# Attention probabilities turned by DMA instead of TensorE, two heads at a time, and the output projection in four parts

## The chip, the cores and the metric

The kernel runs on one core of a Trainium2 chip. The metric is the device time of one execution in microseconds (us); less is better. The engines are TensorE (PE in the profile), VectorE (DVE), ScalarE (ACT), GpSimd (POOL) and SyncE (SP), which issues the DMAs. Each engine has a queue of instructions that it executes in order, and semaphores are all that ties the queues together.

## The reference

One block of a transformer: cross-attention with a residual, then a mixture of experts with a residual. The part that matters, cut down:

```
B, L, D = 8, 128, 256            # T = 128 context tokens; 16 heads of 128, 4 key/value heads
xn = layernorm(x)
q = rope(rms_norm(xn @ wq));  k = rope(rms_norm(xn @ wk));  v = xn @ wv
k_ctx = rms_norm(ctx @ wk_ctx);  v_ctx = ctx @ wv_ctx
k_full, v_full = concat([k_ctx, k]), concat([v_ctx, v])      # 256 keys
scores = q . k_full / sqrt(128) + causal mask on the own keys
probs = softmax(scores);  x1 = x + (probs . v_full) @ wo
xn2 = layernorm(x1)
out = x1 + shared expert(xn2) + top-2 of 8 experts(xn2)
```

## The kernel before, in words

The batch has eight rows b of 128 tokens. Each row has four groups g, one per key/value head, of four query heads each; u = 4b + g counts the groups. Rows 0 and 7 are written out, rows 1 to 6 are a loop on every engine. Behind row 7 comes the tail: router, shared expert and eight experts for two halves of the tokens.

Products keep nearly fp32 precision by splitting each operand into an fp16 high part and an fp16 low part: ScalarE rounds (`..._copy`), VectorE makes the rest (`..._low`, `low()`), and TensorE adds three products. In one group the steps are:

- `scores(b, g)`: four heads against 256 keys into `sc_ps`, with the mask (L1267, L1289).
- VectorE takes the maximum and the bias (L941, L945), ScalarE the four exponentials with their sums `den` (`exps`, L524) into `probs`, fp32.
- `normalise` on VectorE divides `probs` by `den` (L950, L953).
- `turn_probs` (called in the group behind): eight fp32 transposes of 128x128 on PE into `pt_ps` (L1300), `p_copy` and `p_low` round them to `pT_hi` and `pT_lo`.
- `mix`: six matmuls of 512 columns, values stationary, into `o_ps`, which holds the output with the head dimension on the partitions (L1310); `o_copy` and `o_low` round it to `oT_hi`, `oT_lo`.
- `out_proj(b - 1)`: all 48 matmuls of the row before against wo, in group 1 (L1324), into `proj[0]`; then `residual` and, in group 2, `second_norm` on VectorE, with `l2_root` on GpSimd between them.

Between these run the preparations of what comes next: `q_turn` (PE), `q_copy`, `q_low` of the next group; `q` (projection), rotation, `q_squares`, `q_roots`, `q_add` two groups ahead; in group 0 the value projections `vc` and `v`; in group 1 the next row's input: `ln_scale` (DVE), `ln_high` (ACT, L435 with the tile x_hi), `ln_low` (POOL, L712), `turn_inputs` (PE, L1182, L1185), `in_copies`; in group 2 the next row's keys: `kc`, `k`, `k_squares`, `kc_squares`, `k_roots`, `kc_roots`, `kc_scale`, `k_add`, `k_scale`; in group 3 `kc_turn`, `k_turn`, `kc_copy`, `k_copy`, `kc_low`, `k_low`. Every order is written by hand, once per engine, in functions called `row`. There is no planner. `kc` uses the bank `turn`, which all turned inputs and queries share too.

The core of PE's order in group 1 of a row inside the loop:

```
scores(b, 1); q_turn(b, 2); turn_probs(b, 1); q(b, 3)
out_proj(b - 1); turn_inputs(b + 1)
mix(u - 1, 0)
```

## Time and profile before

| | us |
|---|---|
| three runs | 376.12, 376.57, 378.42 (median 376.57) |
| the profiled execution, its own time | 377.97 |
| its span, first to last instruction | 376.3 |
| PE, PE weight loads, DVE, ACT, POOL busy | 343.7, 237.3, 325.6, 271.2, 165.8 |
| mean granted clock of PE | 0.977 |
| DMA, share of 16 engines | 11.0% |

The profile's times come from one execution. PE busy counts matmuls, whose ends are modelled: a matmul's duration holds a tail of about 0.17 us that the next one overlaps, so work on PE is better read from starts than from durations. A granted clock of 1.0 is 2.4 GHz, 0.5 is 1.2 GHz. "Idle before" with an arrow names what ended an engine's wait.

### The profile page before, as it was taken

How to read it: one execution, taken by the hardware profiler on the slowest of the kernel's cores; microseconds unless marked ns; L12 is line 12 of the kernel's file. 1: busy time of each engine (PE TensorE's matmuls, PEld its weight loads, DVE VectorE, ACT ScalarE, POOL GpSimd, SP SyncE). 2: the span in 40 equal slices, each digit the busy share in tenths (PEclk: the TensorE clock that was granted, in tenths of full speed). 3: DMA queues.
4: the chain of work that ended last, by engine and by line, in shares of the span. 5: the costliest groups of instructions: out<-in, count | busy, mean ns of one | idle time of the engine just before them, and what ended most of it. 6: DMA issues, size and time to landing. Idle time of an engine off the chain costs nothing.

```text
span 376.3 us, 7781 instructions
## 1 busy us (share of the span) xinstructions
PE 343.7 (91%) x2471; PEld 237.3 (63%) x2476; DVE 325.6 (87%) x625; ACT 271.2 (72%) x913; POOL 165.8 (44%) x242
## 2 busy tenths in 40 slices
PE   6697798799999999999999999999999999998994
PEld 5373555376567665866685577567666778674572
DVE  1668999998999899899989998999899897759653
ACT  3557879676986797699759876986797567167562
POOL 3356565652754275427344443644174300334330
PEclk9788989999999999999999999999999999989999
DMA  5967000000030003000000000000000000000011
GB/s 179 379 212 223 17 0 2 1 2 14 3 111 0 14 0 111 14 1 0 0 14 0 0 0 14 0 0 0 0 0 1 2 0 2 2 0 3 22 35 57
DMA packets 11603, 13.49 MB, mean 36 GB/s; under 512 B 824, under 2 KB 9024, under 8 KB 11584
## 3 DMA queue, kind: packets, MB, share of 16 engines
q1 hardware_dynamic: 11584, 13.25, 11.0%
q8 instruction: 10, 0.16, 0.2%
q14 instruction: 9, 0.07, 0.1%
HBM read 12.20 MB, written 1.05 MB: 35 GB/s over the span
## 4 chain that ended last, share of the span: by engine, by line
PE 40%; DVE 24%; ACT 17%; issue 10%; POOL 4%; DMA 2%; SPq 1%; DVEq 1%; ACTq 0%; POOLq 0%
PE proj L1324 10%; ACT probs L524 8%; PE pt_ps L1300 5%; DVE probs L953 5%; PE proj L1157 4%; PE turn L1246 3%; DVE nmax L941 3%; DVE pT_lo L879 3%; PE o_ps L1310 3%; POOL q_rot L744 3%; PE sc_ps L1267 2%; ACT pT_hi L435 2%; DMA wq<-in_L_xattn_wq_dram 2%; ACT q_junk L468 2%; DVE q_t L870 2%
## 5 line engine op out<-in xcount | busy, mean ns | idle before, releaser
L524 ACT ACTIVATE probs<-sc_ps,nbias,q_r 128x256 f32<-128x256 f32 x128 | 70.8, 574 | 2.8 <-DVE nbias L945 2.8
L744 POOL TENSOR_TENSOR q_rot<-q_t 128x512 f32<-128x512 f32 x32 | 41.4, 1295 | 42.8 <-DVE q_t L872 42.0
L953 DVE TENSOR_SCALAR probs<-probs,rden 128x256 f32<-128x256 f32 x128 | 51.2, 461 | 1.1
L1157 PE MATMUL proj<-wq_hi,xT 128*128 128x512 f16 x128 | 40.1, 396 | 2.9 <-DVE wq_lo L863 2.9
L435 ACT ACTIVATE pT_hi<-pt_ps 128x512 f16<-128x512 f32 x64 | 34.8, 597 | 10.9 <-PE pt_ps L1300 10.9
L468 ACT ACTIVATE q_junk<-proj 128x128 bf16<-128x128 f32 x128 | 34.0, 295 | 11.7 <-DVE q_t L872 11.7
L879 DVE SCALAR_TENSOR_TENSOR pT_lo<-pt_ps,pT_hi 128x512 f16<-128x512 f32 x64 | 41.0, 682 | 0.6 <-ACT pT_hi L435 0.6
L941 DVE TENSOR_REDUCE nmax<-sc_ps 128x4 f32<-128x1024 f32 x32 | 38.9, 1214 | 1.5 <-PE sc_ps L1289 1.5
L831 POOL TENSOR_TENSOR wq<-xn_all,weight 128x512 bf16<-128x512 f32 x16 | 17.1, 1074 | 44.1 <-DVE weight L1098 23.4
L1324 PE MATMUL proj<-wo_hi,oT_hi 128*128 128x256 f16 x128 | 34.9, 273 | 0.0
L1324 PE MATMUL proj<-wo_lo,oT_hi 128*128 128x256 f16 x128 | 34.9, 273 | 0.0
L1324 PE MATMUL proj<-wo_hi,oT_lo 128*128 128x256 f16 x128 | 34.9, 273 | 0.0
L1300 PE MATMUL pt_ps<-ident,probs 128*128 128x128 f32 x256 | 34.2, 278 | 0.3
L701 POOL TENSOR_TENSOR q_r<-q_me,power 128x4 f32<-128x4 f32 x32 | 33.3, 1042 | 2.5
L435 ACT ACTIVATE qT_hi<-turn 128x512 f16<-128x512 f32 x32 | 19.5, 610 | 19.9 <-PE turn L1246 19.9
L1300 PEld LDWEIGHTS pt_ps<-ident,probs 128*128 128x128 f32 x256 | 29.5, 143 | 0.8 <-DVE probs L953 0.5
L1246 PE MATMUL turn<-ident,q_rot 128*128 128x128 f32 x128 | 19.8, 277 | 10.6 <-POOL q_rot L744 4.9
L468 ACT ACTIVATION_READ_ACCUMULATOR q_junk<-proj 128x1 f32 x128 | 28.5, 227 | 0.0
L524 ACT ACTIVATION_READ_ACCUMULATOR probs<-sc_ps,nbias,q_r 128x1 f32 x128 | 27.6, 215 | 0.0
L1310 PE MATMUL o_ps<-pT_hi,v_hi 128*128 128x512 f16 x64 | 24.3, 379 | 3.2 <-DVE pT_lo L879 3.2
L879 DVE SCALAR_TENSOR_TENSOR oT_lo<-o_ps,oT_hi 128x512 f16<-128x512 f32 x32 | 21.9, 686 | 5.8 <-ACT oT_hi L435 5.8
L1267 PE MATMUL sc_ps<-kT_hi,qT_hi 128*128 128x256 f16 x128 | 24.5, 273 | 0.5 <-ACT probs L524 0.2
(216 smaller groups left out, 920.7 us busy)
## 6 DMA issues: line engine op xcount, KB each, us to landing
wq<-in_L_xattn_wq_dram SPq DMA_DIRECT2D x4, 512.0 KB, 9.1
w<-in_L_ffn_w_dram SPq DMA_DIRECT2D x2, 1024.0 KB, 10.5
wq<-in_L_xattn_wo_dram SPq DMA_DIRECT2D x1, 2048.0 KB, 8.2
ctx_b<-in_ctx_dram SPq DMA_DIRECT2D x8, 128.0 KB, 2.1
out_dram<-x_all SPq DMA_DIRECT2D x4, 256.0 KB, 2.2
x_all<-in_x_dram SPq DMA_DIRECT2D x1, 896.0 KB, 12.3
wkc<-in_L_xattn_wk_ctx_dram SPq DMA_DIRECT2D x1, 512.0 KB, 4.2
wk<-in_L_xattn_wk_dram SPq DMA_DIRECT2D x1, 512.0 KB, 5.1
```

What stands on the lines that cost most here:

```text
L435: return nc.scalar.activation(out_, in_, ACT.Copy, scale=scale)
L468: last = nc.scalar.activation(junk[:, head], bank[:, head], ACT.Square, scale=scale, accum_out=dst[:, h:h + 1])
L524: last = nc.scalar.activation(probs[:, h, :], sc_ps[:, h, :], ACT.Exp, bias=nbias[:, h:h + 1], scale=q_r[:, g, h:h + 1], accum_out=den[:, ...
L701: nc.gpsimd.tensor_tensor(r, me, power[:], ALU.pow).then_inc(root, 1)
L744: nc.gpsimd.tensor_tensor(q_rot[:], q_t1[:], q_t2[:], ALU.add).then_inc(q_added, 1)
L879: return nc.vector.scalar_tensor_tensor(out=lo, in0=src, scalar=scale, in1=hi, op0=ALU.mult, op1=ALU.subtract)
L941: nc.vector.tensor_reduce(nmax[:], sc_ps[:], AX_X, ALU.max, negate=True).then_inc(s_max, 1)
L953: last = nc.vector.tensor_scalar(probs[:, h, :], probs[:, h, :], rden[:, h:h + 1], None, ALU.mult)
L1157: last = nc.tensor.matmul(bank[:], xT[:, a, c, :], w[:, c, cols], start=(n == 0), stop=(n == 3 * DC - 1))
L1300: last = nc.tensor.transpose(pt_ps[:, a, h * P:(h + 1) * P], probs[:, h, a * P:(a + 1) * P], ident[:])
L1310: last = nc.tensor.matmul(o_ps[:], v[:, a, g * P:(g + 1) * P], p[:, a, :], start=(a == 0 and i == 0), stop=(a == 1 and i == 2))
L1324: last = nc.tensor.matmul(proj[0][:, 0:D], o[:, h // R, (h % R) * P:(h % R + 1) * P], w[:, h, :], start=(h == 0 and i == 0), stop=(h == H ...
```

## The change

- ScalarE no longer leaves the probabilities whole: `p_round` rounds `probs`, undivided, to fp16 `p_hi`, two heads at a time; the first pair stands between the third and the fourth exponential. `p_rest` on VectorE makes `p_lo`. `normalise`, `turn_probs` on PE, `p_copy` and `p_low` are gone.
- SP issues four transposing DMAs per group, high and low of each pair (128 x 512 fp16), to `pT_hi` and `pT_lo` (two slots).
- `mix` has the probabilities stationary and 128 columns of values moving: 24 matmuls. Its result has the tokens on the partitions, so that `o_scale` on VectorE divides by `den` there. `o_round` (ACT) and `o_rest` (POOL) round it, two groups behind, and two more DMAs per group turn it to `oT_hi`, `oT_lo`.
- `out_proj` becomes `out_part(b - 1, g)`, 12 matmuls at the end of each group, ahead of `mix(b, g - 1)`, into a bank of its own; `residual` and `second_norm` stand one behind the other in group 3, `l2_root` too.
- `kc` has its own bank; `k` goes ahead of `kc`; `k_add` moves from VectorE to GpSimd; `kc_copy` and `k_copy` move from between the exponentials to behind them; wo, w3 and w2 are loaded in quarters; some tiles of the tail share memory with tiles of the rows; in the tail the four parts stand apart.

The core of the diff:

```
+            def turn_probs(b, g):
+                u = G * b + g
+                slot = u % 2
+                if u >= 2:
+                    sp.wait_ge(pv_done, u - 1)
+                for pair in range(2):
+                    heads = slice(2 * pair, 2 * pair + 2)
+                    for src, dst, split in ((p_hi, pT_hi, p_high), (p_lo, pT_lo, p_low)):
+                        sp.wait_ge(split, 2 * u + 1 + pair)
+                        sp.dma_start_transpose(dst[:, slot, heads].rearrange("p h a t -> p (h a) t"),
+                                               src[:, heads].rearrange("p h k -> p (h k)")).then_inc(d_pT[slot], 16)
+            def turn_out(b, g):
+                u = G * b + g
+                if b:
+                    sp.wait_ge(wo_part, u - G + 1)
+                for src, dst, split in ((o_hi, oT_hi, o_high), (o_lo, oT_lo, o_low)):
+                    sp.wait_ge(split, u + 1)
+                    sp.dma_start_transpose(dst[:, g, :].rearrange("p (h t) -> p h t", h=R),
+                                           src[:, g % 2, :]).then_inc(d_oT[g % 2], 16)
...
+            for b in range(B):
+                for g in range(G):
+                    turn_probs(b, g)
+                    if G * b + g >= 2:
+                        turn_out(*divmod(G * b + g - 2, G))
...
+                    if g == 1 and b + 2 < B:
+                        next_ctx(b + 2)
...
+            def p_round(b, g, pair):
+                u = G * b + g
+                if g or not (isinstance(b, int) and b == 0):
+                    act.wait_ge(*landed(d_pT, b, g - 1))
+                act.wait_ge((s_exp_half, s_exp)[pair], u + 1)
+                heads = slice(2 * pair, 2 * pair + 2)
+                copy(p_hi[:, heads], probs[:, heads], P_SCALE).then_inc(p_high, 1)
...
                 for h in range(R):
-                    if h == R // 2:
-                        for step in between:
-                            step(b + 1)
+                    if h == R - 1:
+                        p_round(b, g, 0)
...
+                    p_round(b, g, 1)
+                    if g == 3 and not last:
+                        kc_copy(b + 1)
+                        k_copy(b + 1)
+                    if g >= 2:
+                        o_round(b, g - 2)
+                    elif not first:
+                        o_round(b - 1, g + 2)
...
+                    if g >= 2:
+                        o_rest(b, g - 2)
+                    elif not first:
+                        o_rest(b - 1, g + 2)
+                    if ahead_of(b, g, 2, last) and g != 2:
+                        q_roots(*ahead_of(b, g, 2, last))
+                    if g == 0 and not last:
+                        ln_root(b + 1)
+                    if g == 3 and not first:
+                        l2_root(b - 1)
...
+            def o_scale(b, g):
+                u = G * b + g
+                dve.wait_ge(pv_done, u + 1)
+                dve.wait_ge(s_rden, u + 1)
+                seen(dve, o_low, u - 1)
+                nc.vector.scalar_tensor_tensor(out=o_n[:, g % 2, :].rearrange("p (h d) -> p h d", h=R),
+                                               in0=o_ps[:].rearrange("p (h d) -> p h d", h=R),
+                                               scalar=O_SCALE / (P_SCALE * V_SCALE),
+                                               in1=rden[:, g % 2, :].unsqueeze(2).broadcast_to([P, R, P]),
+                                               op0=ALU.mult, op1=ALU.mult).then_inc(o_scaled, 1)
...
+                    if g == 3 and not first:
+                        residual(b - 1)
+                        second_norm(b - 1)
...
+            def mix(b, g):
+                u = G * b + g
+                seen(pe, o_scaled, u)
+                cols = slice(g * P, (g + 1) * P)
+                pe.wait_ge(*landed(d_pT, b, g))
                 for a in range(2):
                     for h in range(R):
+                        for i, (p, v) in enumerate(((pT_hi, v_hi), (pT_hi, v_lo), (pT_lo, v_hi))):
+                            last = nc.tensor.matmul(o_ps[:, h * P:(h + 1) * P], p[:, g % 2, h, a, :], v[:, a, cols],
...
+            def out_part(b, g):
+                pe.wait_ge(*landed(d_oT, b, g))
...
                     if g == 1:
-                        if not first:
-                            out_proj(b - 1)
                         if not last:
                             turn_inputs(b + 1)
...
+                    if not first:
+                        out_part(b - 1, g)
                     if g:
-                        mix(u - 1, g - 1)
+                        mix(b, g - 1)
```

## Rows read from the trace of the kernel before

**Rows 1.** Stretches: us, busy PE, PEld, DVE, ACT, POOL, then clock, DMA share, GB/s

```profile
29.14:68.07 38.93, 33.45 (x197) 20.78 (x198) 36.94 (x65) 33.11 (x114) 24.43 (x29) 0.91 0.19 59
...
141.03:176.54 35.51, 34.27 (x249) 23.76 (x248) 33.85 (x69) 28.39 (x108) 18.02 (x28) 1.00 0.11 33
...
283.20:308.02 24.82, 23.98 (x179) 17.01 (x178) 23.04 (x47) 16.21 (x54) 6.16 (x9) 1.00 0.00 1
```

**Rows 2.** Chain of waits in one row: start, us, what

```profile
151.42 5.24 PE proj L1324 x48
...
157.11 1.29 PE o_ps L1310 x6
...
174.43 0.99 ACT q_junk L468 x7
```

**Rows 3.** Order of time around group 1: start, us, engine, line, operation

```profile
149.09 1.04 PE L1300 MATMUL pt_ps<-ident,probs 128*128 128x128 f32 x8
...
156.50 0.27 PE L1182 MATMUL turn<-ident,x_hi 128*128 128x128 f16 x2
...
158.24 0.38 PE L1267 MATMUL sc_ps<-kT_hi,qT_hi 128*128 128x256 f16 x2
...
159.72 0.22 PE L1289 MATMUL sc_ps<-causal,identb 128*128 128x128 bf16 x1
159.77 0.61 PE L1246 MATMUL turn<-ident,q_rot 128*128 128x128 f32 x4
...
149.60 1.21 DVE L941 TENSOR_REDUCE nmax<-sc_ps 128x4 f32<-128x1024 f32 x1
...
151.13 0.57 ACT L524 ACTIVATE probs<-sc_ps,nbias,q_r 128x256 f32<-128x256 f32 x1
...
153.30 0.44 ACT L435 ACTIVATE x_hi<-xs 128x256 f16<-128x256 f32 x1
...
153.81 0.67 POOL L712 TENSOR_TENSOR x_lo<-xs,x_hi 128x256 f16<-128x256 f32 x1 [4.03 <-ACT x_hi L435]
```

**Rows 4.** Groups of instructions by form: busy us, mean ns, idle before

```profile
L953 DVE TENSOR_SCALAR probs<-probs,rden 128x256 f32<-128x256 f32 x128 | 51.2, 461 | 1.1
L744 POOL TENSOR_TENSOR q_rot<-q_t 128x512 f32<-128x512 f32 x32 | 41.4, 1295 | 42.8 <-DVE q_t L872 42.0
...
L1300 PE MATMUL pt_ps<-ident,probs 128*128 128x128 f32 x256 | 34.2, 278 | 0.3
...
L930 DVE TENSOR_TENSOR k_sum<-k_t 128x512 f32<-128x512 f32 x8 | 8.4, 1053 | 0.0
...
L863 DVE SCALAR_TENSOR_TENSOR wq_lo<-wq,wq_hi 128x1024 f16<-128x1024 f32 x4 | 5.1, 1271 | 3.3 <-ACT wq_hi L435 3.2
...
L435 ACT ACTIVATE wq_hi<-wq 128x1024 f16<-128x1024 f32 x4 | 4.2, 1056 | 3.3 <-DMA wq<-in_L_xattn_wq_dram 3.3
```

**Rows 5.** Order of time on ScalarE and GpSimd, groups 1 to 3

```profile
158.47 0.55 POOL L694 TENSOR_TENSOR ln_rs<-ln_ve,power 128x1 f32<-128x1 f32 x1
...
166.12 1.01 POOL L701 TENSOR_TENSOR kc_r<-kc_me,power 128x4 f32<-128x4 f32 x1
...
167.17 1.14 ACT L435 ACTIVATE kc_n<-turn,kc_r 128x128 f32<-128x128 f32 x4
...
172.05 0.70 ACT L435 ACTIVATE kT_hi<-turn,kw_scaled 128x512 f16<-128x512 f32 x1
```

**Rows 6.** DMA issues (KB each, median us to landing) and one issue on SP's queue

```profile
ctx_b<-in_ctx_dram SPq DMA_DIRECT2D x8, 128.0 KB, 2.1
...
121.62 0.33 SPq L410 DMA_DIRECT2D ctx_b<-in_ctx_dram  x1
```

**Rows 7.** Stretches and PE in order of time around an idle PE

```profile
48.40:51.80 3.40, 3.40 (x14) 2.18 (x13) 3.37 (x4) 2.21 (x6) 2.36 (x1) 0.52 0.00 0
...
47.78 0.66 PE L1246 MATMUL turn<-ident,q_rot 128*128 128x128 f32 x4 [2.56 <-DVE cT_lo L879]
48.25 1.90 PE L1300 MATMUL pt_ps<-ident,probs 128*128 128x128 f32 x8
```

More of the change, by code:

```diff
@@ L588, in row @@
                         q_squares(*ahead_of(b, g, 2, last))
+                    if g == 2 and not last:
+                        kc_scale(b + 1)
                     if first and g == 3:
@@ L593, in row @@
                     if g == 0:
+                        vc_copy(b)
                         v_copy(b)
-                    if (g or not first) and not (g == 3 and last):
-                        o_copy(u - 1, (g - 1) % G)
-                    if g == 2 and not last:
-                        kc_scale(b + 1)
-                        k_squares(b + 1)
-                    if g == 0:
-                        vc_copy(b)
                     if first and g == 1:
@@ L1020, in row @@
                         ln_scale(b + 1)
-                    if g or not first:
-                        p_low(u - 1)
-                    if g == 2 and not first:
-                        second_norm(b - 1)
+                    if g >= 2:
+                        o_scale(b, g - 2)
+                    elif not first:
+                        o_scale(b - 1, g + 2)
+                    if g == 2 and not last:
+                        k_turn(b + 1)
                     if ahead_of(b, g, 2, last):
@@ L1029, in row @@
                         dve.wait_ge(ln_stat, b + 2)
+                    inv_den(b, g)
+                    if g == 0 and not last:
+                        ln_gather(b + 1)
                     if g == 2 and last:
@@ L1116, in e_hidden @@
                                         ALU.mult).then_inc(e_hid, 1)
-            p_low(G * B - 1)
+            o_scale(B - 1, G - 2)
             turned(w3T[:, half_e[1]], proj[1][:].bitcast(BF16), t_w3b, r_w3b)
-            xn_copy(2)
-            o_low(G * B - 1, G - 1)
             dve.wait_ge(c_low, 1)
             dve.wait_ge(d_sh, 80)
-            for part in range(4):
+            for part in range(2):
+                router(0, part)
+            xn_copy(2)
+            o_scale(B - 1, G - 1)
+            for part in range(2, 4):
                 router(0, part)
@@ L1169, in project_ctx @@
                     for c in range(DC):
-                        last = nc.tensor.matmul(bank[:], a[:, c, :], w[:, c, :], start=(i == 0 and c == 0),
+                        last = nc.tensor.matmul(bank, a[:, c, :], w[:, c, :], start=(i == 0 and c == 0),
                                                 stop=(i == len(terms) - 1 and c == DC - 1))
@@ L1396, in row @@
                         q_turn(*ahead_of(b, g, 1, last), last)
-                    if g or not first:
-                        turn_probs(b, g)
+                    if g == 2 and not last:
+                        k(b + 1)
                     if first and g < 2:
```

326 lines of the change are left out of this document (159 added, 167 removed).

## The prediction, made before the change was run

> **What bounds the kernel now.** I read the views from coarse to fine: first the engines over one batch row, then the chain of waits, then the order of time in one group, and last the tensor clock. The looped rows repeat every 35.5 us (141.03 to 176.54: PE busy 34.3, VectorE 33.9, ScalarE 28.4, GpSimd 18.0), and the clock is full [rows 1]. So two engines stand at 95% and nothing else is near. The chain of waits passes in one row from PE to VectorE and back; its largest piece is the output projection, 48 matmuls in one block of 5.24 us [rows 2]. What to see there beside its length is its place: it stands between the projections of group 1 and `turn_inputs`, and it keeps PE at work while the next row's input is still being made [rows 3].
>
> **What the change removes.** PE drops 32 fp32 transposes per row. Eight in one group span 1.04 less the last one's tail of 0.17, or 0.87 us: 3.5 us per row [rows 3, 4]. VectorE drops 16 divisions per row (128 take 51.2 us: 6.4) and `k_add` (1.1) [rows 4]. The rounding stays: `p_round` is 512 columns from fp32 and half of the 1.06 us that 1024 take, 0.5 us as the PSUM copy was; `p_rest` is half of the 1.27 us of `wq_lo`, 0.6 us, as `p_low` was [rows 4]. Its other bound is the 1.05 us that an fp32 addition of two SBUF tiles takes on VectorE; I take 0.6, since `wq_lo` is the same operation with the same kinds of operand, and leave +3.6 us of VectorE work per row (8 x 0.45) for the range. `mix` becomes 24 matmuls of 128 columns where it was 6 of 512; two fp16 operations of 128 columns span 0.27 where one spans 0.22, so 0.055 us each and 1.32 in all against 1.29 [rows 2, 3]: nothing. GpSimd gains `k_add` and four `o_rest`, each like `q_add`, 1.29 us: +6.5 on 18.0; `o_scale` is on VectorE what `o_low` was, 0.6 [rows 1, 4]. By sums alone PE would stand at 30.8, ScalarE at 28.4, VectorE at 26.4, GpSimd at 24.5. If nothing waited, a row would take 31, not 35.5.
>
> Edits with one answer, all at nothing: the context projection in its own bank (it only frees `turn`), `k` ahead of `kc`, the shared tiles for `xn2T`, `ahead` and `tied` (their waits are for casts long done), the weights in quarters. On SP the next context and the quarters of w3 and w2 now stand behind waits for `p_rest` and `o_rest`; who reads them comes most of a row later. In row 0 the first transposes stand behind 1 MB of wo: up to 3 us, once.
>
> **What it moves, and the waits that come.** I walked one row after the change through the six queues: every instruction starts when its queue has issued the one ahead of it and 0.05 us after the last event that it waits for (ScalarE's `x_hi` ends at 153.74, GpSimd starts at 153.81 [rows 3]). The same walk of the kernel before gives 35.8 against 35.5 measured, so I trust it to half a microsecond. It gives 38.2 after. The loop that sets it runs once around the row in six legs:
>
> 1. VectorE, group 0: maximum, bias, `q_low`, `o_scale(b-1,2)`: 1.25 + 0.1 + 0.6 + 0.7 = 2.7. `mix(b-1,3)` waits for that; before, `o_low` had cleared the bank in the group ahead.
> 2. PE: `mix` 1.3, `v` 1.3, a quarter of the output projection 1.31, scores 1.53 and their tail 0.17: 5.7 [rows 2, 3].
> 3. Group 1: maximum and bias 1.45, three exponentials, `p_round` and the fourth 2.66 (each 0.54 from 151.13 on), `ln_high` 0.44, `ln_low` 0.67, events: 5.4 [rows 3]. Only then may `turn_inputs(b+1)` go. Before, the next input was ready at 154.48 (153.81 and 0.67), and PE came to it at 156.50, because the 5.24 us stood ahead of it. Now only `q_turn` and `q` (0.44 + 1.3) stand ahead: **PE is idle 3.7 us**, and behind it on PE wait the quarter, `mix(b,0)` and the scores of group 2.
> 4. PE: `turn_inputs` 0.44, quarter 1.31, `mix` 1.3, scores 1.7: 4.8.
> 5. Group 2: maximum and bias 1.5, exponentials and first rounding 2.9, `p_round` and `o_round` 1.0, `k_squares` 1.0, on GpSimd `k_roots` and `kc_roots` 1.3 + 1.4, then `kc_scale` 1.04 and `q_copy` 0.5: 10.8 [rows 2, 5].
> 6. Group 3: exponentials and rounding 2.9, `p_round` 0.5, the two key copies 1.1, `o_round` 0.6, on GpSimd `o_rest` 1.25 and `q_roots` 1.3, `l2_root` 0.9 (its second half 0.55), and `second_norm` 0.3: 8.9 [rows 4, 5]. `second_norm` now stands directly behind `residual` on VectorE, and behind it the next row's maximum, 2.5 us late. Before, a group lay between them, and the key copies stood between the exponentials (172.05) [rows 5], so PE also waits 1.4 us at the row's first scores.
>
> The legs make 38.3, 2.5 more than the same walk of before. The probabilities by DMA are not in this loop: with 0.45 us per issue (0.33 for a plain one) and 2.1 us to landing for 128 KB [rows 6] the last of the four lands about 9 us after its scores, `mix` comes at 10 to 12.
>
> **The clock.** Where PE had been idle 2.56 us (to 47.78), its granted clock was 0.52 from 48.4 to 51.8, and eight transposes took 1.90 instead of 1.04 [rows 3, 7]. 3.4 us at the lower level, 1.2 GHz instead of 2.4, cost 1.7 us of work. An idle time of 3.7 us in every row is longer than that one. The 4.8 us of leg 4 follow at once and are on the loop, so I add 1.4 (bounds 0, if no dip follows, and 3.4, if the 2.1 us before `mix(b-1,3)` bring a second).
>
> **The sum.** Profiled execution: 377.97 us (span 376.3, 1.7 around it). Rows 1 to 6: 6 x (2.5 + 1.4) = +23.4. Row 0: VectorE is busy 36.9 of 38.9 us there and sheds 7, its input for row 1 is made ahead of the exponentials, and part is lost to the weights' transfers: -3 (0 to -6) [rows 1]. Row 7 has no `turn_inputs`: its legs from first to last maximum make 21.5 where 24.8 stood: -3.3 [rows 1]. End of the scores to the end of the last `mix`: three quarters of the projection come in (3.9), two blocks of transposes go (1.7): +2.2. Behind it the projection's last quarter and its 0.7 + 0.6 + 1.3 + 2.5 us chain through o_scale, o_round, o_rest and DMA hide behind the shared expert, and the wait for the second norm shows: 10.0 us to the last `turn_xn2` as before. Sum +19.3: 397.3, and since this execution lies 1.4 above the median of the runs (376.57), **396 us**.
>
> **The transposes.** The trace has no transpose by DMA, so rows bound it: each holds the queue for 0.33 us (an issue) to 2.1 us (issue to landing of 128 KB, if each waits for the one ahead) [rows 6]. I take 0.45 and 2.1 to landing, nearer the lower end, since plain loads of this trace overlap; both ends stay for the range. The Trainium skill (Advanced Engine Details and Errata, X-Bar Transpose) has such DMAs as fast as plain ones on Trainium2, 350 to 400 GB/s, by estimate 0.35 us for 128 KB; by it the sum stays as it is. No run here shows it yet.
>
> **The rivals.**
> - *Clock holds.* The walk without dips: 6 x 1.4 less, 388 us. For it: with 1.2 us idle in a row of 35.5 PE keeps its clock at 1.00 [rows 1]. Against it: the one idle time of that length that rows show [rows 7].
> - *The DMA queue becomes the bound.* Six transposes per group and one input per row: from 1.55 us of queue per DMA on, 24 of them exceed the 38 of the walk. At 1.8 us a row takes 43.6, +8.1 over 7 rows, 433 us; at 2.1 it is 50.8, 484 us. For it: nothing in the trace shows a transpose at the plain rate. Against it: a plain issue takes 0.33 us [rows 6]. The Trainium skill (VectorE: DVE Perf Modes, The three transpose paths) speaks against the change here: 1309 ns by DMA for a block of 128x128, 390 ns on TensorE. If the 24 blocks of a group did not overlap, that would be 31 us per group by estimate, far beyond the upper end; no row shows it.
> - *Faster: the sums win.* If the loop were slack (the walk overstates legs 5 and 6, or events come earlier), PE's 30.8 plus its 3.7 us wait, less 0.8 for an earlier maximum, would make 33.7, -1.8 x 6 - 4 = -15, so 362 us. For it: both full engines are relieved. Against it: leg 3 alone, made of measured durations.
> - *No change.* The wait of leg 3 takes what the transposes and divisions give, and legs 1, 5 and 6 are half hidden: 376 us.
>
> **How the numbers follow.** Forecast 0.42, clock holds 0.24, DMA bound 0.16, faster 0.10, no change 0.08. The measurement tells about 1% apart. The range 372 to 433 takes in the no-change case, both bounds of the clock and the slow `p_rest` (7 rows of 3.6 more: 421), and leaves out the faster case and the upper half of the DMA case (0.08), about 0.18. Faster 0.10, same 0.09, slower 0.81: forecast, clock and DMA cases and the edges of no change.
>
> **What would show it.** In the changed profile: row period 38 to 40 us; PE idle about 3.7 us before `turn_inputs`, released by GpSimd's `x_lo`; PE busy near 31 of that period; clock 0.5 for some 3 us in each row right behind it; VectorE's first maximum of a row waiting behind `second_norm`; VectorE waits for GpSimd's root. Wrong if `turn_inputs` does not wait, if SP's queue is full or `mix` waits for a DMA in every group (DMA case), if the period is under 35.5 or if `p_rest` takes over 0.9 us.

## The result and the profile after

The changed kernel takes 434.6 us (median of 4 runs, 433.3 to 435.5) against 376.9 (376.1 to 378.4): ratio 1.152, 95% interval 1.147 to 1.158. The direction was forecast, the size was not: the forecast was 396 us, and its range ended at 433.

The first view is the page of the changed kernel: busy time by engine, then groups (line, form, count, then busy us and mean ns, then idle time before) and DMA issues.

```profile
PE 341.2 (79%) x2796; PEld 246.1 (57%) x2796; DVE 300.2 (69%) x489; ACT 273.2 (63%) x913; POOL 228.6 (53%) x282
...
L822 POOL TENSOR_TENSOR q_rot<-q_t 128x512 f32<-128x512 f32 x32 | 48.3, 1510 | 42.4 <-DVE q_t L954 42.4
L961 DVE SCALAR_TENSOR_TENSOR p_lo<-probs,p_hi 128x512 f16<-128x512 f32 x64 | 63.8, 1034 | 0.3
...
pT_lo<-p_lo SPq DMA_TRANSPOSE x64, 2.5
```

VectorE is busy 25 us less than before and PE 2.5 us less, and still no engine is busy for more than 79% of the span: the time is in waits. The stretches show where (us, busy PE, PEld, DVE, ACT, POOL, clock, DMA share, GB/s). A row is counted from its first maximum to that of the next. The lines are row 0, row 1, one steady row (row 5), row 7 up to its last maximum, and all behind that.

```profile
27.64:68.82 41.18, 29.98 (x215) 19.63 (x216) 34.76 (x50) 33.06 (x113) 28.48 (x30) 0.88 0.50 108
68.82:117.79 48.97, 38.03 (x292) 27.54 (x291) 33.73 (x52) 29.18 (x108) 30.33 (x35) 0.84 0.42 83
244.21:285.74 41.53, 34.53 (x293) 24.79 (x292) 29.83 (x50) 28.47 (x107) 23.40 (x28) 0.95 0.41 79
326.88:351.01 24.13, 20.51 (x193) 16.09 (x191) 20.75 (x31) 16.20 (x53) 9.80 (x9) 0.93 0.47 84
351.01:433.80 82.79, 65.29 (x496) 46.42 (x494) 46.62 (x93) 36.77 (x55) 21.93 (x23) 0.89 0.18 37
```

Against before [rows 1]: the first maximum 1.5 us earlier; row 0 41.2 for 38.9; rows 2 to 6 209.1 for 177.7 (41.5 for 35.5 when steady); row 7 24.1 for 24.8; behind the last maximum 82.8 for 68.3. Row 1 is the surprise: 49.0 for 37.4. In all -1.5 + 2.3 + 11.6 + 31.4 - 0.7 + 14.5 = 57.6, the difference of the spans (433.8 - 376.3) but for rounding.

Order of time in the steady row, around group 1 (start, duration, engine, line, operation):

```profile
256.97 0.41 ACT L493 ACTIVATE x_hi<-xs 128x256 f16<-128x256 f32 x1
...
257.31 1.77 DVE L961 SCALAR_TENSOR_TENSOR p_lo<-probs,p_hi 128x512 f16<-128x512 f32 x2
...
257.46 1.07 POOL L778 TENSOR_TENSOR x_lo<-xs,x_hi 128x256 f16<-128x256 f32 x1 [3.50 <-ACT x_hi L493]
...
258.76 0.29 PE L1264 MATMUL turn<-ident,x_hi 128*128 128x128 f16 x2 [3.97 <-POOL x_lo L778]
...
259.48 0.42 PE L1392 MATMUL pt_ps<-wo_hi,oT_hi 128*128 128x256 f16 x1
...
283.96 0.18 DVE L1053 BATCH_NORM_AGGREGATE ln_mv<-ln_st 128x2 f32<-128x6 f32 x1
285.24 0.41 DVE L1057 TENSOR_SCALAR xn_all<-x_all,ln_mv,ln_rs  x1 [1.09 <-POOL ln_rs L760]
285.74 1.23 DVE L1025 TENSOR_REDUCE nmax<-sc_ps 128x4 f32<-128x1024 f32 x1
```

PE reaches `turn_inputs` (L1264) early and stands 3.97 us for `x_lo`, which in [rows 3] was ready before PE came. The first matmuls behind it take 0.42 us where the same ones take 0.27 elsewhere in the row, since the granted clock (the third number from the end) is down:

```profile
258.70:262.10 3.40, 3.34 (x19) 2.55 (x20) 0.81 (x2) 1.62 (x8) 3.32 (x4) 0.53 0.47 91
```

I call such a stretch a dip. At the row's end the next maximum starts at 285.74, right behind the second norm, which waited 1.09 us for GpSimd's root.

The four groups of this row, from maximum to maximum, take 8.46, 12.59, 8.51 and 11.97 us. These numbers are the measure for the experiments.

### The profile page after: what moved, and what is told of

Read it like the earlier page. It is cut to its first block, busy times and chain, and to the rows that moved or that the text cites. A ratio compares the mean times of both kernels' runs of the same rounds, so it can differ in the third digit from the quotient of the medians.

```text
span 433.8 us, 8856 instructions
## 1 busy us (share of the span) xinstructions
PE 341.2 (79%) x2796; PEld 246.1 (57%) x2796; DVE 300.2 (69%) x489; ACT 273.2 (63%) x913; POOL 228.6 (53%) x282
## 3 DMA queue, kind: packets, MB, share of 16 engines
HBM read 12.20 MB, written 1.05 MB: 31 GB/s over the span
## 4 chain that ended last, share of the span: by engine, by line
issue 30%; POOL 26%; ACT 15%; PE 12%; DVE 10%; DMA 3%; SPq 2%; POOLq 0%; ACTq 0%; DVEq 0%
ACT probs L590 7%; POOL q_rot L822 5%; POOL o_lo L809 5%; POOL q_r L767 4%; DVE nmax L1025 3%; ACT p_hi L493 2%; POOL k_sum L795 2%; DMA wq<-in_L_xattn_wq_dram 2%; PE pt_ps L1392 1%; ACT o_hi L493 1%; PE proj L1557 1%; DVE p_lo L961 1%; DVE nbias L1029 1%; POOL kc_r L767 1%; POOL q_me L765 1%
## 5 line engine op out<-in xcount | busy, mean ns | idle before, releaser
L961 DVE SCALAR_TENSOR_TENSOR p_lo<-probs,p_hi 128x512 f16<-128x512 f32 x64 | 63.8, 1034 | 0.3
L1025 DVE TENSOR_REDUCE nmax<-sc_ps 128x4 f32<-128x1024 f32 x32 | 39.1, 1222 | 35.7 <-PE sc_ps L1366 35.5
L1379 PE MATMUL o_ps<-v_hi,pT_hi 128*128 128x128 f16 x256 | 49.4, 232 | 16.1 <-DVE o_n L1000 12.4
L809 POOL TENSOR_TENSOR o_lo<-o_n,o_hi 128x512 f16<-128x512 f32 x32 | 40.2, 1256 | 35.8 <-ACT o_hi L493 35.8
L1379 PE MATMUL o_ps<-v_lo,pT_hi 128*128 128x128 f16 x256 | 49.3, 232 | 0.0
L1379 PE MATMUL o_ps<-v_hi,pT_lo 128*128 128x128 f16 x256 | 49.1, 231 | 0.0
L493 ACT ACTIVATE p_hi<-probs 128x512 f16<-128x512 f32 x64 | 40.5, 633 | 3.4 <-DMA pT_lo<-p_lo 1.1
L1392 PE MATMUL pt_ps<-wo_hi,oT_hi 128*128 128x256 f16 x128 | 39.2, 306 | 0.0
L1379 PEld LDWEIGHTS o_ps<-v_hi,pT_hi 128*128 128x128 f16 x256 | 26.9, 105 | 21.4 <-issue 15.7
L1392 PE MATMUL pt_ps<-wo_lo,oT_hi 128*128 128x256 f16 x128 | 38.9, 304 | 0.0
L1392 PE MATMUL pt_ps<-wo_hi,oT_lo 128*128 128x256 f16 x128 | 38.9, 304 | 0.0
L795 POOL TENSOR_TENSOR k_sum<-k_t 128x512 f32<-128x512 f32 x8 | 11.1, 1389 | 42.0 <-DVE k_t L954 41.9
```

Source lines behind the costliest of these rows:

```text
L493: return nc.scalar.activation(out_, in_, ACT.Copy, scale=scale)
L809: nc.gpsimd.tensor_tensor(o_lo[:, g % 2, :], o_n[:, g % 2, :], o_hi[:, g % 2, :], ALU.subtract).then_inc(o_low, 1)
L961: return nc.vector.scalar_tensor_tensor(out=lo, in0=src, scalar=scale, in1=hi, op0=ALU.mult, op1=ALU.subtract)
L1025: nc.vector.tensor_reduce(nmax[:], sc_ps[:], AX_X, ALU.max, negate=True).then_inc(s_max, 1)
L1379: last = nc.tensor.matmul(o_ps[:, h * P:(h + 1) * P], p[:, g % 2, h, a, :], v[:, a, cols], start=(a == 0 and h == 0 and i == 0), stop=(a = ...
L1392: last = nc.tensor.matmul(out_ps, o[:, g, h * P:(h + 1) * P], w[:, g * R + h, :], start=(g == 0 and h == 0 and i == 0), stop=(g == G - 1 a ...
```

## The experiments

Fifteen variants of the changed kernel were run and one of the kernel before. Nothing is left out of the computation except where the expectation says so. Code is cut to the lines that matter. By cover I mean work that PE has ahead of a wait: while PE does it, the input that it would wait for becomes ready.

**The next row's input behind its cover.**

```
-                        if not last:
-                            turn_inputs(b + 1)
...
                     if g:
                         mix(b, g - 1)
+                    if g == 1 and not last:
+                        turn_inputs(b + 1)
```

> The changed kernel with turn_inputs(b+1) moved behind the output quarter and mix(b,0) of group 1; nothing left out. Theory (lost cover): in the changed kernel PE stands idle 4.0 us before turn_inputs (254.8 to 258.8), with the quarter and mix waiting behind it and the clock at half for the 3 us after. With 2.6 us of work ahead of it the idle time falls to 1.4 us, no dip follows, and the maximum of group 2 comes 4.3 us earlier: row period 41.5 to 37.2, 434.6 to about 407 us. Rival 1 (groups 2 and 3 or the DMA set the row, the idle time is slack): period stays within 0.5 us of 41.5 and the time above 430. Rival 2 (only the idle time goes, the clock dips elsewhere): period 38.9, 418 us.

407.1 us (405.2 to 408.8; ratio 1.084, 1.078 to 1.089): 27.4 us less for one moved call. In the steady row group 1 went from 12.59 to 8.28 us, and the other groups stayed within 0.2; over the six rows group 1 alone gives 27 us. PE in order of time, and the clock of the stretch behind (second fence):

```profile
238.43 0.28 PE L1264 MATMUL turn<-ident,x_hi 128*128 128x128 f16 x2 [1.34 <-POOL x_lo L778]
238.55 0.27 PE L1264 MATMUL turn<-ident,x_lo 128*128 128x128 f16 x2
```

```profile
238.40:241.80 3.40, 3.37 (x30) 2.68 (x31) 1.96 (x3) 2.13 (x9) 3.32 (x4) 1.00 0.48 93
```

An idle time of 1.34 us is left, and the clock stays at 1.00. The loss of the cover is shown, with its size.

**The clock alone.**

```
                     if g == 1:
+                        if not last and not first:
+                            seen(pe, o_scaled, G * b)
+                            keep_warm(56)
                         if not last:
                             turn_inputs(b + 1)
```

> The changed kernel with 56 idle matmuls of 128 columns (3.0 us at full clock) into the head outputs' bank ahead of turn_inputs, behind the wait for o_scale that mix(b,0) has anyway; nothing is left out, the 4.0 us until x_lo stay. Theory (the dip behind the idle time is on the path): the quarter and mix take 2.6 instead of about 4.3 us, row period 41.5 to 39.8, 434.6 to about 424 us. Rival (clock off the path, or another dip takes its place): 41.5 and 433 to 436 us. If the filler itself delays turn_inputs, PE's wait for x_lo is gone and the period grows.

424.1 us (423.6 to 425.2), 10.5 less. Group 1 of the steady row takes 11.12 instead of 12.59 us, so the dip costs 1.47 us there. Behind `turn_inputs` the clock is full:

```profile
250.90:254.30 3.40, 3.40 (x50) 3.23 (x47) 0.61 (x2) 1.43 (x7) 3.32 (x4) 1.00 0.54 104
```

Of the 27 us of the lost cover some 10 were clock. The dips are not all of one length. In row 3 of the changed kernel group 1 takes 14.09 us, 1.5 more than in the steady row, behind nearly the same wait for `x_lo` (4.3 us), and the clock is down for 6.8 us (from 173.6) instead of 3.4:

```profile
174.10:180.10 6.00, 5.56 (x39) 4.76 (x40) 1.19 (x2) 2.00 (x11) 4.74 (x6) 0.50 0.75 162
```

With the filler that row's group 1 takes 11.31 us, so the longer dip was what set it apart.

**The same loss made in the kernel before.** Here only the two calls of group 1 change places, with none of the new DMAs.

```
-                        if not first:
-                            out_proj(b - 1)
                         if not last:
                             turn_inputs(b + 1)
+                        if not first:
+                            out_proj(b - 1)
```

> The kernel before, with only turn_inputs(b+1) moved ahead of the whole output projection of group 1; no work changed. Theory (the 5.24 us of the projection are the cover of the next row's input): PE, which now starts the projection at 151.26, waits there for x_lo until 154.48, 3.2 us, and runs the next 3 us at half clock; PE is 97% busy, so nearly all of it is added: 3.5 to 4.9 us in each of six rows, 376.6 to 398 to 406 us. So this one move alone, without any of the new DMAs, makes about half of the change's loss. Rival (VectorE and the probabilities set the row, PE's wait is slack): under 383 us.

404.3 us (403.1 to 406.5; ratio 1.075, 1.069 to 1.080). Waits by cause (us in total, times, longest):

```profile
PE turn L1182 <- POOL x_lo L712: 19.8, 6, 3.3
```

There are six waits of 3.3 us, one per row. In rows 2 to 5 the clock falls behind them, and group 1 takes 15.5 us for 10.4; in rows 1 and 6 the wait is as long, the clock stays full, and group 1 takes 13.8. The first 4 us behind the waits of rows 4 and 6:

```profile
202.50:206.50 4.00, 3.81 (x24) 2.85 (x25) 2.09 (x4) 1.72 (x10) 2.38 (x3) 0.62 0.13 33
284.00:288.00 4.00, 4.00 (x39) 3.63 (x40) 1.93 (x4) 1.53 (x8) 2.21 (x3) 1.00 0.00 0
```

So the wait is sure and the dip is not. One swap of the order costs half of what the whole change does.

**The second norm off the next maximum.**

```
                     if g == 3 and not first:
                         residual(b - 1)
+                    if g == 3 and last:
                         second_norm(b - 1)
...
+                    if g == 0 and not first and norm:
+                        second_norm(b - 2)
```

> The changed kernel with second_norm(b-1) moved from the end of group 3 into group 0 of the next row, behind o_scale, on VectorE; nothing left out. Theory (the norm's wait for GpSimd's root stands ahead of the next row's maximum): in the changed kernel the scores end at 283.95 in the row of 244 to 286 and the maximum starts at 285.74; here it starts right behind them, group 3 takes 10.3 instead of 12.0 us, in 6 rows 10 us: about 424.5 us. Rival (group 3 is set by kc, the key copies or the roots on the other engines and the maximum only shows it): under 0.5 us per row, above 431 us.

428.5 us (427.8 to 430.9), 6.1 less where 10 less was expected. In the steady row group 3 fell by 1.2 (11.97 to 10.78) and group 0 rose by 0.36 (by 1.0 in rows 3 and 6). The stretch that holds the row's first scores tells why:

```profile
275.80:278.90 3.10, 3.03 (x15) 2.18 (x16) 2.39 (x7) 0.60 (x1) 1.92 (x4) 0.50 0.45 87
```

In the changed kernel the clock of the same place (283.00 to 286.00) is 1.00; here it is 0.50. The norm was on the path, and a dip gave part of it back. PE's waits for the keys ahead of it (1.25 and 0.72 us) are those of the changed kernel; why the clock falls here and not there stays open. Of the gain in this profile 2.9 us lie in group 0 of row 1, which the edit does not touch and which differs from run to run (below, at the weights).

**Who slows p_rest.** Two runs. In the first `q_add` on GpSimd is replaced:

```
-                nc.gpsimd.tensor_tensor(q_rot[:], q_t1[:], q_t2[:], ALU.add).then_inc(q_added, 1)
+                nc.gpsimd.tensor_tensor(pw_o[:], pw_i[:], power[:], ALU.pow).then_inc(q_added, 1)
```

> The changed kernel with GpSimd's q_add (an fp32 addition of two 128x512 tiles, 1.27 to 1.72 us) replaced by a power of a 128x4 tile (1.0 us by its rows); this leaves out the sum of the two rotation products, queries become a constant. Theory (GpSimd and VectorE slow each other when both work on SBUF tiles): in the changed kernel p_rest takes 0.68 us where GpSimd stands and up to 1.76 beside q_add; here its mean falls from 1.03 to about 0.7, and the row gets shorter by 0.4 (x_lo) + 0.7 (group 3) to 1.8 us with q_add's own 0.3 to 0.7: 434.6 to between 422 and 428. Rival (p_rest is slow of itself, two SBUF sources and a 16-bit one, or because of the transposing DMAs): mean stays at 0.9 or more, and only q_add's own time shows, under 3 us.

In the second the low parts are rounded and waited for as ever, but not transposed:

```
                         sp.wait_ge(split, 2 * u + 1 + pair)
+                        if dst is pT_lo:
+                            continue
```

> The changed kernel without the 96 transposes by DMA of the low parts (p_lo and o_lo; PE multiplies the high part in their place, so the output lacks those products); the engines' own instructions and waits stay. Theory (the queue, 24 issues of 1.27 us in a row of 41.5, is not what sets rows 1 to 6; only row 7 and the tail wait for a landing): row period within 0.5 us of 41.5, mean of p_rest unchanged at 1.0, row 7 and the tail 3 to 5 us shorter, 434.6 to about 430 us. Rival (DMA queue bound): period down by 3 us or more, under 412 us. Rival for p_rest (slowed by the transposing DMAs): its mean falls toward 0.8.

Groups by form, first of the run without `q_add`, then of the run without low transposes:

```profile
L965 DVE SCALAR_TENSOR_TENSOR p_lo<-probs,p_hi 128x512 f16<-128x512 f32 x64 | 45.3, 746 | 0.3
```

```profile
L965 DVE SCALAR_TENSOR_TENSOR p_lo<-probs,p_hi 128x512 f16<-128x512 f32 x64 | 63.3, 1026 | 0.3
```

With half of the transposing DMAs gone, the mean is 1026 ns, as in the changed kernel (1034). With GpSimd's addition gone it is 746. So `p_rest` is an operation of 0.68 us that takes up to 1.76 us beside GpSimd. On the path this is worth less than I expected: the run without `q_add` takes 428.5 us (427.7 to 429.7), 6.0 less, and in the steady row only group 3 changed, by 0.56. This run also spares a part of `q_add`'s own time, so the 6.0 us need not all come from the meeting of the two. Without the low transposes the kernel takes 433.6 us (433.3 to 434.4) and a steady row 41.5: the DMA queue does not set the rows. The 3 to 5 us that I expected behind them did not come either; row 7 is 0.8 us shorter, the stretch behind the last maximum (83.1 us) is as long as in the changed kernel.

**GpSimd's large subtraction of the weights.** In the changed kernel, at the start of row 1 (VectorE, then GpSimd):

```profile
70.06 4.03 DVE L1029 TENSOR_TENSOR nbias<-nmax,q_r 128x4 f32<-128x4 f32 x1
...
70.01 4.06 POOL L879 TENSOR_TENSOR wo_lo<-wq,wo_hi 128x2048 f16<-128x2048 f32 x1
```

A bias of 128x4 elements, 0.16 us elsewhere, lasts until GpSimd ends, and with it stand the exponentials and the whole group.

```
-                    if first and g == 3:
+                    if g == 1 and b_is(b, 1):
                         pool.wait_ge(wo_high, 4)
                         nc.gpsimd.tensor_tensor(wo_lo[:, own_wo, :], wo32[:, own_wo, :], wo_hi[:, own_wo, :],
                                                 ALU.subtract).then_inc(wo_low2, 1)
```

> The changed kernel with GpSimd's 4.06 us subtraction wo_lo (128x2048) moved from the end of row 0 to group 1 of row 1, where GpSimd and VectorE stand idle, and its wait on PE moved to the third quarter; nothing left out. Theory (beside it VectorE's bias of 128x4 took 4.03 instead of 0.16 us, and the whole of group 0 of row 1 waited): row 1 falls from 49.0 to about 43, 434.6 to about 428.5 us. Rival (the bias is not on the path, row 1 is long for another reason): bias at 0.16 but row 1 above 47, time within 2 us of 434.6.

The bias is back at 0.17 us and row 1 takes 41.8 instead of 49.0; the whole kernel takes 429.9 us (429.7 to 430.3), 4.7 less. Part of the gain does not arrive: rows 2 and 5 of that profile are 0.9 and 1.2 us longer than in the changed kernel's, and row 3 is 1.2 shorter. The difference lies in group 1, where the clock tells it: it is down for 6.9 us in rows 2 and 5 and for 3.4 in row 3. Why one dip is longer than another no run shows.

Not all of row 1's loss is the bias. Group 0 of that row takes 15.19 us in the changed kernel, where PE waits 3.7 us for `o_scale`, which stands behind the late bias, and the clock is then down (0.51 from 74.50 to 81.00). In the run with `turn_inputs` behind its cover the wait is 3.7 us too, the clock stays at 1.00 behind it, and the group takes 12.30. Up to 3 us of the total of any run in which this subtraction stays in its place can come from there.

**Behind the last maximum.** Three runs. The order on VectorE and ScalarE, cut:

```
+                    if g == 3 and last:
+                        xn_copy(1)
+                        turned(w1T[:, half_e[1]], ...)
                     inv_den(b, g)
...
+                        o_scale(B - 1, G - 2)
                     if g == 3 and not first:
                         residual(b - 1)
...
             gate_exp(0)
+            o_round(B - 1, G - 2)
```

> The changed kernel with the order behind the last maximum altered: on VectorE the copy of the second block for the gate and w1's half ahead of the last inverse and p_rest, o_scale of group 2 ahead of the last residual and norm; on ScalarE the gate's exponential ahead of o_round of group 2. Nothing left out. Theory (the tail's +12 us over what was forecast is mostly PE waiting for casts that stand behind others on VectorE and ScalarE: gate logits 3.8 us later than before, ScalarE's gate exponential behind o_round, which waits for an o_scale behind the norm): logits 1.7 us earlier and 3 to 4 us off the wait for the exponential, 434.6 to about 429.5 us. Rival (the tail hangs on the transposes of the last probabilities and outputs, 4 + 2 of 1.3 us each): within 2 us of 434.6.

433.4 us (430.5 to 434.5), the rival's number. The gate's waits are gone, as expected, and another stands in their place. PE, then SP's queue in order of time:

```profile
365.16 0.40 PE L1393 MATMUL pt_ps<-wo_hi,oT_hi 128*128 128x256 f16 x1 [4.33 <-DMA oT_lo<-o_lo]
```

```profile
357.91 1.26 SPq L449 DMA_TRANSPOSE pT_hi<-p_hi  x1
359.22 2.00 SPq L449 DMA_TRANSPOSE pT_lo<-p_lo  x1
361.31 1.21 SPq L458 DMA_TRANSPOSE oT_hi<-o_hi  x1
362.57 1.26 SPq L458 DMA_TRANSPOSE oT_lo<-o_lo  x1
```

The issue at 362.57 lands 2.5 us later, and only then PE goes on. These are four of 14 issues (not 16, as I wrote below) that stand end to end from 346.88 to 366.46. Then both edits together, this order and no low transposes:

> The changed kernel with both edits that alone brought about 1 us: the altered order behind the last maximum, and no transposes by DMA of the low parts (the output lacks the products with p_lo and o_lo). Theory (behind the last maximum two chains stand side by side, the casts on VectorE and ScalarE and the DMA queue, which issues 16 transposes end to end from 346.9 to 366.5 in the run with the altered order; each covers the other): the last mix starts 12 to 13 us after the last maximum instead of 17.5, total about 427 us. Rival (the tail hangs on a third chain, PE's own work or the second norm): 432 to 433.5 us, as each alone.

427.4 us (424.1 to 428.8). Alone they brought 1.2 and 0.9, together 7.1. The last `mix` starts 12.6 us after the last maximum, for 19.2 in the changed kernel and 17.5 with the order alone. There are two chains of nearly the same length, and each hides the other.

**What an issue costs.** Two transposes of 128x1024 in place of four of 128x512:

```
-                for pair in range(2):
-                    heads = slice(2 * pair, 2 * pair + 2)
...
+                    sp.wait_ge(split, 2 * u + 2)
+                    sp.dma_start_transpose(dst[:, slot].rearrange("p h a t -> p (h a) t"),
+                                           src[:].rearrange("p h k -> p (h k)")).then_inc(d_pT[slot], 16)
```

> The changed kernel with two transposes of 128x1024 per group in place of four of 128x512, each started when both halves are rounded; nothing left out. Theory (the queue's time goes by bytes: 1.27 us for 128x512): 2.5 us per issue, landing 3.7 us after issue, the last landing 1.3 us later than now; steady rows unchanged within 0.5 us, row 7 and the tail 2 to 5 us longer, about 437 us. Rival (1.27 us is a fixed cost of an issue): 1.3 us per issue, the queue half empty, row 7 and the tail as short as without the low parts or shorter, 430 to 433 us.

My theory, that the time goes by bytes, fell. All issues of this line (ns min, median, max):

```profile
L447 SPq DMA_TRANSPOSE pT_hi<-p_hi x32: 1232/1232/2233, 33.9 to 353.0; - x32
L447 SPq DMA_TRANSPOSE pT_lo<-p_lo x32: 1231/1274/1347, 35.3 to 354.3; - x32
...
DMA to landing us min/median/max: 3.0/3.2/3.6
```

With 128x512 an issue takes the queue 1.26 us (median of `pT_lo`), with 128x1024 1.27: between these two sizes it is a fixed cost. Landing grows only from 2.5 to 3.2 us. The time is 433.3 us (431.0 to 435.7), no difference that can be told from none. That the casts cover the gain in the tail fits the runs above, but this run does not show it.

**Together.** The moves of the input, the norm, `wo_lo` and the tail's order at once:

> The changed kernel with four moves at once: turn_inputs behind the quarter and mix, second_norm in the next row's group 0, wo_lo in group 1 of row 1, the order behind the last maximum. Nothing left out. Theory (they are separate waits, their prices add): 434.6 less 27.5, 10, 2 (row 1 is already short once turn_inputs is moved) and 5: about 390 us, row period 35.5 to 36. Rival (the next chain, through k_roots, kc_roots and kc_scale in groups 2 and 3, takes over): period 37, about 400 us. Faster than the kernel before only if the period falls under 35.

398.2 us (396.5 to 400.1; ratio 1.057), the rival's number. Rows 2 to 6 take 36 to 37 us, and group 3 still 10.5. With `turn_inputs` moved once more, behind the scores of group 2:

> As the run with four moves, but turn_inputs stands behind the scores of group 2, and cT_low behind that group's maximum. Theory: the 1.5 us that PE still waits for x_lo are covered and the scores of group 2 come 2 us earlier, but the exponentials of group 2 stand behind the input's copies and q_copy on ScalarE, so the row gains only 0.5 us: 398.2 to about 395 us. Rival (the scores of group 2 were the limit): 2 us per row, 386 us. Rival (the keys of the next row come later, and groups 2 and 3 hang on them): no gain or a loss.

406.9 us (405.4 to 407.9), a loss of 8.7. In the steady row group 1 fell to 6.4 us and group 2 rose to 11.5: PE now waits 2.4 us for `cT_lo`, the context part of this input, from which the next row's keys start. Too much cover is a loss too. I went back to the first place and put the key copies where the kernel before has them:

```
                     if h == R // 2 - 1:
                         last.then_inc(s_exp_half, 1)
+                        if keys:
+                            kc_copy(b + 1)
+                            k_copy(b + 1)
```

> The run with four moves (398.2 us), plus the two key copies of the next row between the exponentials of group 3 on ScalarE, and kc_low and k_low ahead of the inverse and p_rest on VectorE, as the kernel before has them. Nothing left out. Theory (PE's waits at the row's first scores, 1.2 us for kT_hi and 0.7 for kT_lo, and VectorE's late maximum, are these copies' place behind the exponentials): group 3 falls from 10.5 to 8 to 9 us, in 6 to 7 rows 10 to 15 us: about 386 us. Rival (group 3 is set by kc_scale and the turns ahead of the copies): under 0.5 us per row, above 394 us.

391.2 us (390.4 to 392.3), 7.0 less than 398.2, where 10 to 15 were expected. Group 3 is 9.5 us, and a steady row 35.3, about that of the kernel before (35.5). No wait of PE for `kT_hi` or `kT_lo` is left in the row. PE is busy for 31.3 us of it; its longest waits are 1.7 us ahead of a `mix`, for the landing of `pT_lo`, and 1.3 for `x_lo`. Which chain now keeps the row at 35.3, no run tested.

> As the run with the key copies between the exponentials, and two transposes of 128x1024 per group in place of four of 128x512. Theory (an issue costs 1.25 us whatever its size, so the queue is relieved of 64 of 192 issues, which shows where it is full, in row 7 and behind the last maximum): rows 1 to 6 within 0.3 us of the run beside it, row 7 and the tail 3 to 5 us shorter, about 382 us. Rival (the later start of the first half's transpose costs what the queue gains): within 1.5 us of the run beside it.

With two transposes per group as well, it takes 386.5 us (385.9 to 387.7). The rows are the same within 0.5 us, and the stretch behind the last maximum is 3.3 us shorter: where the queue is full, fewer issues pay. Two runs are left, the weights without GpSimd, and the tail once more:

```
-                        nc.gpsimd.tensor_tensor(wo32[:, own_wo, :], wo32[:, own_wo, :],
-                                                scale_w[:].unsqueeze(2).broadcast_to([P, H // 2, D]),
-                                                ALU.mult).then_inc(wo_scaled, 1)
...
+                        wo_split(2)
+                        wo_split(3)
```

> The 386.5 us version (four moves, key copies, two transposes per group) with GpSimd's two large operations on the output weights taken away: ScalarE scales all four quarters itself, and VectorE subtracts the last two in group 1 of row 1 (two of 1.21 us by the rows of the first two). Nothing left out. Theory (beside a GpSimd operation on a 128x2048 tile VectorE stands: the bias of 128x4 takes 3.20 us in row 0 instead of 0.16): that bias is back at 0.2 to 0.4, row 0 3 us shorter, 386.5 to about 383 us, although VectorE has 2.4 us of work more. Rival (row 0 waits for the weights or ScalarE, and the bias only shows it): within 1 us of 386.5.

385.6 us (384.6 to 387.2), ratio 1.027, where the run ahead of it had 1.028. Row 0 fell from 40.6 to 38.8, the bias in it from 3.19 to 0.16 us, and row 1 rose by 0.5: the mechanism is shown, but there is no gain in all that the measurement can tell.

```
             out_part(B - 1, 0)
+            mix(B - 1, G - 1)
...
             out_part(B - 1, 3)
+            shared_up(0)
```

> As the run beside it, and behind the last maximum: the last mix directly behind the first output quarter, its o_scale and o_round ahead of the copies of w3, the shared expert's first products behind the last output quarter instead of ahead. Nothing left out. Theory (the chain mix, o_scale, o_round, o_rest, transpose, last quarter, norm sets the end, and the 3.5 us that PE stands before the last norm halve its clock for the gate logits, 3.3 instead of 1.9 us): mix 3.4 us earlier, logits 1.4 us shorter, 4 to 5 us in all, about 378.5 us. Rival (the DMA queue, full to the issue of oT of group 2 at 319, gives the gain back): 1 us or less.

382.8 us (380.8 to 383.4), ratio 1.019 (1.014 to 1.024), the best version of the changed kernel, and still 2% slower than the kernel before. The gain of 2.8 us lies between the two numbers expected. The last gate logits take 1.92 instead of 3.25 us, the last `mix` starts 10.0 us after the last maximum instead of 14.5, and PE then waits 0.6 us for `oT_lo` and 1.9 for the tokens: part of the gain is given back. In this profile rows 1 to 6 together take 216.0 us for 215.1 in the kernel before, and rows 0 and 7 are 0.9 and 1.1 shorter; what is still longer is the stretch behind the last maximum, 73.0 us for 68.3. No run was faster than the kernel before.

## Why the prediction was right in direction and wrong in size

The profile of the changed kernel lies 38.2 us above the sum: 12.3 behind the last maximum, 7.6 in row 1, 11.9 in rows 2 to 6, 5.3 in row 0 and 2.6 in row 7, less 1.5 ahead of row 0. Two steps of the prediction failed: row 1 was taken for a steady row, and the tail was summed and not walked. In the steady row the mechanism held, and the sizes were too small.

**Legs 1 and 2** (2.7 + 5.7 = 8.4 us): measured 8.46. Right.

**Legs 3 and 4 and the clock.** The mechanism is right. PE's idle time was forecast at 3.7 us and measured at 3.97; the dip was forecast at 1.4 and measured at 1.47 by the filler. Group 1 came out at 12.6 where 10.2 + 1.4 = 11.6 was forecast: `x_lo` takes 1.07 us beside `p_rest`, not 0.67, and its end came 5.85 us behind the maximum, not 5.4. The rival in which the clock holds is out, but the argument for the dip was weaker than it looked: in the swapped kernel before, the same idle time of 3.3 us brought a dip in four rows and none in two. The sign "PE busy near 31" also hangs on the clock: PE is busy for 34.5 us of the steady row, and for 31.4 in the run in which the clock stays full there.

**Legs 5 and 6** (10.8 + 8.9 = 19.7): measured 8.5 + 12.0 = 20.5 as groups 2 and 3. The border of the two legs is the first exponential of group 3; counted so they take 11.3 and 9.2 us. The loop is the one I walked: moving the norm shortens group 3, and moving the key copies shortens it again once the norm is gone. Of the 0.8 that were missing, 0.56 went with GpSimd's addition. A steady row is 41.5 against 38.2 + 1.4 = 39.6.

**p_rest, a term that was mis-sized.** I took 0.6 us because `wq_lo` has the same operands, and left the rest for the range. It takes 0.68 with GpSimd idle and 1.03 in the mean, over the 0.9 that I had named as a sign of being wrong. Rows that would have warned me were in the kernel before: `nbias`, 0.16 us elsewhere, took 1.38 us at 49.40 and 2.18 at 69.33, each time beside a GpSimd operation on the weights. I had counted GpSimd's added work (+6.5 us per row) as time of GpSimd alone. The Trainium skill (SBUF — State Buffer, SBUF: two separate sides) says that a VectorE operation with two SBUF inputs and a GpSimd operation that reads SBUF lock each other out for a whole instruction. The trace agrees: 4.03 us for a bias beside 4.06 on GpSimd, while `q_low`, which reads one of its inputs from PSUM, stays at 0.68 to 0.69.

**The sum of rows 1 to 6** was +23.4, measured +42.9. Missing are 10.4 in rows 2 to 6 (2.1 each), 1.5 more in row 3, where the dip lasted longer, and 7.6 in row 1. Row 1 is the first step that failed: I multiplied one walked row by six, and put at nothing what still reaches into row 1 from row 0. GpSimd's `wo_lo` and the first bias of row 1 met in the kernel before too (VectorE, then GpSimd):

```profile
69.33 2.18 DVE L945 TENSOR_TENSOR nbias<-nmax,q_r 128x4 f32<-128x4 f32 x1
...
67.02 4.46 POOL L798 TENSOR_TENSOR wo_lo<-wq,wo_hi 128x2048 f16<-128x2048 f32 x1
```

There `wo_lo` starts 1.05 us ahead of the row's first maximum, after the change 1.19 us behind it, so that the bias stands for nearly all of it. In neither profile does it wait for a load: it starts as soon as GpSimd is through with the root ahead of it, so it was GpSimd's work ahead of it that moved it, and not the loads in quarters. With `wo_lo` out of the way row 1 takes 41.8 us, against 37.4 + 3.9 = 41.3 forecast. Whether the edits to the loads come at nothing, no run shows.

**Row 0**, -3 forecast, +2.3 measured. It has two causes: GpSimd's scaling of the weights held the bias of group 2 for 3.20 us, and group 3, at 13.4 us for 9.7, waits for `kc_scale` (3.1 us on PE), which is the chain of legs 5 and 6 in a row that I had credited with VectorE's freed work. The first is shown by the run without it; the second and larger one is read from the trace alone.

**Row 7**, -3.3 forecast, -0.7 measured. In its profile `mix` waits 2.0 us for the landing of `pT_lo` and 1.3 for `o_scale`, and `p_round` 0.4 for a landing. Without the low transposes the row is 0.8 shorter; the rest of the 2.6 was not taken apart.

**The tail**, +2.2 forecast, +14.5 measured, is the other step that failed and the largest part of the miss. From the last maximum to the end of the last `mix` it is 20.6 us for 9.4, +11.2: I had added up PE's work (+3.9 - 1.7) on an engine that was not the limit. The casts for the gate stand behind two `p_rest`, the gate's exponential behind an `o_round` that waits for an `o_scale` behind the second norm, and SP's queue is full there. Behind that the forecast nearly held as far as the last turn for the norm, 11.1 us against 10.2. The last 2.4 us lie behind this turn, where I had put nothing: 1.6 of them are the gate logits, 3.56 us for 1.93, at a clock of 0.50. I had walked the row and only summed the tail.

**The DMA queue.** 0.45 us per issue was forecast, 1.26 is measured, under the 1.55 from which I had it bind: 24 x 1.26 + 0.58 = 31 us of a row of 41.5. It was right that the queue does not set rows 1 to 6, and wrong to leave it out of the tail: behind the last maximum the issues stand end to end. I had priced this rival for all rows or none. The Trainium skill (Advanced Engine Details and Errata, X-Bar Transpose) has transposes as fast as plain DMAs: for the landing the trace nearly agrees (2.5 us against 2.3 for a plain 128 KB in the same profile), for the queue it does not (1.26 against 0.58). The Trainium skill (VectorE: DVE Perf Modes, The three transpose paths) gives 1309 ns for one block of 128x128. Here four blocks landed 2.5 us after their issue and eight blocks 3.2, where 1309 ns for each in turn would make 5.2 and 10.5 by estimate; so the blocks do overlap, as the forecast needed.

## What to carry to other kernels

A block of work that stands between a wait and what it feeds is cover, and to split it is to spend it: before a long block is cut up, read from the order of time what becomes ready beneath it. Work moved to GpSimd is priced by what it does to VectorE's operations on SBUF beside it, in the rows where the two meet, and not by GpSimd's own free time. Walk the first row and the tail as the steady row is walked: half of this miss lay in the tail and in row 1, where sums had stood in for a walk. And where two chains are of equal length, as in this tail, each repair alone looks worthless.

## What the runs showed of the hardware

- A transpose by DMA from SBUF to SBUF held SP's queue for 1.26 us in the median at 128x512 and for 1.27 at 128x1024 (single ones for over 2 us); it landed 2.5 and 3.2 us after its issue.
- A GpSimd subtraction on a 128x2048 tile held a VectorE operation on 128x4 elements for 4.03 of its 4.06 us. A VectorE operation of 0.68 us on 128x512 elements, with both inputs in SBUF, took 1.03 us in the mean and up to 1.76; `q_low`, of the same size with one input in PSUM, stayed at 0.69.
- PE's idle time alone does not tell whether its clock falls. Behind 3.97 us it ran the next 3.4 us at 0.53, and behind 3.3 us it fell in four rows of one run and stayed at 1.00 in two. Behind 1.34 us it kept its clock in one place, and behind 1.25 and 0.72 us it fell in another.
